# One planned transformer layer on one core: the table of landing times behind the static order is made longer

## The reference, cut to what matters

```
q, k, v = x @ Wq, x @ Wk, x @ Wv              # q and k rotated (rope)
a = softmax(q1 k1' * s + mask) - lam * softmax(q2 k2' * s + mask)
o = a @ v ; group norm over (tokens, 64) of each head ; o @ Wo
x = layernorm(x + o)
W' = clip(round(W / mean|W|), -1, 1) * mean|W|  # W_up, W_gate, W_down
x = layernorm(x + (silu(x @ W_up') * (x @ W_gate')) @ W_down')
```

## Time and profile before

| | |
|---|---|
| median of 3 runs | 2376.57 us (2372.23 to 2381.06) |
| profiled execution, own time | 2373.91 us |
| its span in the trace | 2372.1 us |
| mean granted TensorE clock | 0.989 of full |
| PE busy | 2235.5 us (94%) |
| DVE, ACT, POOL busy | 1715.7 (72%), 1466.9 (62%), 1169.2 us (49%) |
| DMA | 256.54 MB, mean 108 GB/s |

### The profile page before, as it was taken

One profiled execution on the slowest core, in us unless ns is written; L12 is line 12 of the kernel. 1 busy time (PEld: TensorE's weight loads), 2 busy tenths in 40 slices (PEclk: granted clock), 3 DMA queues, 4 the chain that ended last, 5 costly groups with the idle time before them and its releaser, 6 DMA issues.

```text
span 2372.1 us, 41358 instructions
## 1 busy us (share of the span) xinstructions
PE 2235.5 (94%) x13602; PEld 1399.2 (59%) x13602; DVE 1715.7 (72%) x3829; ACT 1466.9 (62%) x3458; POOL 1169.2 (49%) x1919
## 2 busy tenths in 40 slices
PE   8898998989899999999999999999999999999998
PEld 5555565656566666666666666566656666544443
DVE  3676788888778778888877887887777878632343
ACT  1576667666566767676767776677766777521232
POOL 0465657566546545655654454665444454421232
PEclk9899999999999999999999999999999999999999
DMA  6767465656433121424252223252233111102000
GB/s 225 202 208 199 143 208 177 196 182 204 147 100 113 54 74 57 136 72 129 82 162 78 78 80 84 69 168 68 67 121 101 43 52 39 63 23 84 1 18 18
DMA packets 258004, 256.54 MB, mean 108 GB/s; under 512 B 31360, under 2 KB 199424, under 8 KB 255744
## 3 DMA queue, kind: packets, MB, share of 16 engines
q1 hardware_dynamic: 246016, 220.26, 31.0%
q10 hardware_dynamic: 11776, 33.63, 4.5%
HBM read 182.53 MB, written 71.30 MB: 107 GB/s over the span
## 4 chain that ended last, share of the span: by engine, by line
PE 60%; DVE 8%; issue 4%; ACT 3%; POOL 3%; DMA 0%; DVEq 0%; POOLq 0%; ACTq 0%; SPq 0%
PE F L1045 16%; PE F L1032 9%; PE F L1054 8%; PE PV L986 8%; PE S L969 7%; PE F L949 6%; PE F L1012 4%; DVE e_long L1315 2%; ACT dt_long L1103 1%; ACT e_long L1113 1%; DVE e_long L1386 1%; POOL linv L1243 1%; DVE e_short L1386 1%; PE F L953 1%; DVE th L1364 1%
## 5 line engine op out<-in xcount | busy, mean ns | idle before, releaser
L1243 POOL TENSOR_TENSOR linv<-lsum,powers 128x2 f32<-128x2 f32 x512 | 410.5, 802 | 503.0 <-ACT e_long L1113 381.9
L1113 ACT ACTIVATE e_long<-e_long,nmax 128x768 f32<-128x768 f32 (+3 forms) x512 | 504.1, 988 | 127.9 <-DVE nmax L1315 123.8
L1315 DVE CUSTOM_DVE_ANT_0 e_long<-S,mask_b 128x768 f32<-128x768 f32 (+3 forms) x512 | 511.2, 1020 | 95.0 <-PE S L969 90.8
L969 PE MATMUL S<-kstk,qstk 128*128 128x384 f32 (+5 forms) x1536 | 496.8, 421 | 25.7 <-DVE nmax L1315 21.9
L1103 ACT ACTIVATE dt_long<-F 128x512 f32<-128x512 f32 (+3 forms) x544 | 258.5, 516 | 241.1 <-PE F L949 235.3
L969 PEld LDWEIGHTS S<-kstk,qstk 128*128 128x128 f32 x1536 | 274.8, 191 | 164.7 <-issue 83.3
L1386 DVE SCALAR_TENSOR_TENSOR e_long<-e_long,coef 128x1024 f32<-128x1024 f32 (+3 forms) x256 | 277.2, 1083 | 78.1 <-POOL coef L1244 77.5
L1012 PE MATMUL F<-xT,wr 128*128 128x512 f32 x640 | 309.5, 615 | 10.7 <-ACT dt_long L1103 6.8
L1113 ACT ACTIVATE e_short<-e_short,nmax 128x384 f32<-128x384 f32 (+3 forms) x512 | 283.5, 558 | 37.0 <-DVE nmax L1315 36.1
L1256 POOL TENSOR_TENSOR hid<-th,hid 128x512 f16<-128x512 f32 x128 | 148.3, 1159 | 299.4 <-ACT hid L1156 163.8
L1315 DVE CUSTOM_DVE_ANT_0 e_short<-S,mask_b 128x384 f32<-128x384 f32 (+3 forms) x512 | 235.2, 487 | 65.4 <-PE S L969 62.9
(11 more groups left out here) (110 smaller groups left out, 3259.3 us busy)
## 6 DMA issues: line engine op xcount, KB each, us to landing
qstk<-dq SPq DMA_DIRECT2D x512, 128.0 KB, 2.8
dq<-hl SPq DMA_DIRECT2D x32, 1024.0 KB, 4.8
wr<-in_w_proj ACTq DMA_DIRECT2D x48, 512.0 KB, 4.1
kstk<-dk SPq DMA_DIRECT2D x64, 256.0 KB, 5.6
da<-ra SPq DMA_DIRECT2D x32, 512.0 KB, 3.2
at_sb<-da SPq DMA_DIRECT2D x32, 512.0 KB, 4.0
dk<-hl SPq DMA_DIRECT2D x8, 1024.0 KB, 4.7
wt<-in_w_up SPq DMA_DIRECT2D x16, 512.0 KB, 6.2
```

Source lines behind the costliest of these rows:

```text
L969: last = nc.tensor.matmul(slot[:, h, :], qstk[:, duo % 4, 2 * r + m, :].bitcast(F32R), kstk[:, g % 2, m, h * w:(h + 1) * w].bitcast(F32R), ...
L1113: nc.scalar.activation(e, e, ACT.Exp, bias=nmax[:, u % 8:u % 8 + 1], scale=-1.0, accum_out=lsum[:, n % 4, m:m + 1]).then_inc(s_exp, 1)
L1243: link(nc.gpsimd.tensor_tensor(linv[:, a % 8, :], lsum[:, a % 4, :], mone, ALU.pow))
L1315: nc.vector.tensor_tensor_reduce(out, slot, mask, -1.0, -NEG, ALU.add, ALU.min, nmax[:, u % 8:u % 8 + 1]).then_inc(s_negmax, 1)
```

## The change

Two tables of the planner get larger numbers. Nothing else is edited: the same instructions are issued, and what changes is their order on each engine.

```
-HAND_OVER = {"pe": .2, "act": .3, "dve": .2, "pool": .2}
-LANDS = {"load q": 3.1, "load k": 5.5, "load v": 4.5, "store v": 3.9, "store rotated": 5.2, "store a": 3.5, "load a": 4.4,
-         "store out": 2.5, "load wo": 4.0, "load x1": 6.0, "load weight": 4.5, "load x": 3.7, "load w": 4.2, "load rope": 5.0, "load lambda": 5.0, "load first": 2.5}
+HAND_OVER = {"pe": .3, "act": .4, "dve": .3, "pool": .3}
+LANDS = {"load q": 4.5, "load k": 7.5, "load v": 6.0, "store v": 7.0, "store rotated": 6.0, "store a": 4.5, "load a": 6.5,
+         "store out": 2.5, "load wo": 9.0, "load x1": 8.0, "load weight": 12.0, "load x": 6.5, "load w": 6.5, "load rope": 5.0, "load lambda": 6.0, "load first": 2.5}
```

## The result

| | before | changed |
|---|---|---|
| median | 2376.57 us | 2351.28 us (2348.82 to 2355.24, 6 runs) |
| profiled execution, own time | 2373.91 us | 2349.49 us |
| mean granted clock | 0.989 | 0.992 |

The ratio is 0.9895, with a 95% interval of 0.9879 to 0.9911: 25.3 us less by the medians, 24.4 by the profiled executions. The forecast was 2356 us, 21 us less, in a range of 2335 to 2380.

The account below looks back on a forecast made before the run. PE, 94% busy, was taken as the bound, with its idle time and lower clock before 620 us to win. Terms -21 + 1 - 1 = -21 us, from the runs' median 2376.6, gave about 2356 us, range 2335 to 2380.

Parts of the forecast that it names:

- The bound: PE, 94% busy, bounds the kernel; what can be won is 71 us idle and 22 us by clock before 620 us.
- Load weight, -21 us: Batch 0's attention: a later planned landing ends ACT's 17 waits for weight pieces; -21 us, bounds 0 and -28.
- four gaps: PE idle behind ACT's late weight pieces in batch 0: 3.79, 3.45, 5.64 and 2.82 us, together 15.7 us.
- the 25.9 us: Idle time plus clock loss on PE behind the weight waits, of which a share of 0.8 was taken as won.
- the 10.2: Us lost to half clock on PE in the stretches behind the first three gaps, 3.4 us each.
- Load q, load k, store rotated: +1 us: Ahead of the first scores: PE's 1.51 us wait goes, but attention starts up to 4 us later; -1.5 to +4.
- the items put at 0: Store v, loads of x, w, x1 and lambda: no PE wait for them seen; 0, bounds -2 and +4.
- Load a, store a, load wo: -1 us: Ahead of the Wo products: two PE waits go, -3.5 us, longer holes cost 2.5 us; bounds -3.5 and +6.
- Hand-overs: 0, bounds -12 and +12: Every hop of a step planned 0.1 us longer: small waits go or PE is late; 0 taken.
- The waits move: Weight waits vanish but ACT, PE and DVE meet elsewhere in batch 0; 0 to -11 us, 2366 to 2377; chance 0.22.
- The scores come late: Longer hops put scores behind more filling and DVE starves; slower, +11 us if its waits double, up to 2400; chance 0.11.
- The small waits go too: Margins take a third of batch 0's other idle time and clock dips: another -22 us, some 2334; chance 0.15.

Follow-up runs that it names:

- e9: The kernel before with only SP's list changed: each load of a weight piece issued three items earlier; 2357.61 us, ratio 0.9920.
- e4: The kernel before with all landing times of the change except load weight, hand-overs as before; 2384.70 us, ratio 1.0030.
- e3: The kernel before with only the hand-overs raised by 0.1 us; 2388.22 us, ratio 1.0054.
- e1: The kernel before with only load weight raised from 4.5 to 12.0; 2366.38 us, ratio 0.9956.
- e5: The kernel before with load weight at 12.0 and the raised hand-overs, all other landing times old; 2361.72 us, ratio 0.9932.
- e2: The changed kernel with load weight set back to 4.5; 2375.38 us, ratio 0.9988.
- e6: The kernel before with all landing times of the change, load weight included, and hand-overs as before; 2363.99 us, ratio 0.9947.
- e12: The changed kernel with load weight at 8.0 and each load of a weight piece issued two items earlier on SP's list; 2344.95 us, ratio 0.9863.

## Why the prediction was right, point by point

**The bound.** PE's idle time in batch 0 is what moved, as forecast: 17.4 of the 24.4 us lie there. The counts of instructions on the engines are as before. PE's longest wait between 60 and 620 us was 5.64 us and is now 2.15.

**Load weight, -21 us.** This is shown. The waits fell from 38.6 us to none, and the edit is worth 12.0 to 26.5 us in four settings, 20.8 in the mean. With the lists of the four engines held fixed (e9) it is 19.6 us. The sum of the term was near the truth, but its two parts were not sized alike. In the four pairs of the table, by one trace of each kernel, PE's idle time falls by 9.7, 19.2, 12.4 and 18.8 us, 15.0 in the mean, where I had summed 15.7 from four gaps; its busy time changes by +2.1, -5.5, -12.8 and -8.5, 6.2 less in the mean, where I had put 10.2 on the clock.

e9 has the same list on PE as the kernel before, so the two can be laid side by side. Its page has:

```profile
span 2354.8 us, 41358 instructions
...
PE 2230.9 (95%) x13602; PEld 1394.7 (59%) x13602; DVE 1715.7 (73%) x3829; ACT 1465.3 (62%) x3458; POOL 1172.9 (50%) x1919
```

PE's idle time is 123.9 us for 136.6, its busy time 4.6 us less: 17.3 of the 25.9 us came home in this pair of traces, 0.67 of it, where I took 0.8. (The medians are 19.6 us apart; the profiled execution of the kernel before had a clock of 0.989, its other runs lie between 0.984 and 0.989.) Laid side by side item by item, the four gaps gave 3.6, 3.4, 5.5 and 2.1 us, 14.6 in all (from the start of the item ahead of a gap to that of the item behind it, in the one trace and in the other). The stretches behind the first three, from the first product behind the wait to the same later product, stand thus in the kernel before and in e9:

```profile
82.63:89.86 7.23, 7.03 (x41) 5.22 (x42) 2.52 (x7) 4.99 (x14) 3.21 (x5) 0.57 0.01 1
111.83:120.32 8.49, 6.19 (x27) 5.08 (x27) 5.95 (x13) 7.03 (x17) 3.32 (x6) 0.60 0.90 298
210.01:215.82 5.81, 5.81 (x9) 2.50 (x10) 1.28 (x1) 3.34 (x9) 1.27 (x3) 0.55 0.60 141
```

```profile
80.90:86.03 5.13, 4.55 (x41) 3.14 (x42) 3.02 (x10) 5.13 (x14) 4.15 (x5) 1.00 1.04 242
105.23:112.49 7.26, 4.46 (x26) 3.05 (x27) 6.58 (x16) 6.80 (x17) 4.36 (x6) 1.00 1.07 282
197.32:200.57 3.25, 3.25 (x9) 1.52 (x10) 3.05 (x10) 1.84 (x4) 1.27 (x3) 1.00 1.04 300
```

The lower clock is gone from all three, but they are shorter by 2.1, 1.2 and 2.6 us, 5.9 in all, not 10.2. Two things were wrong in the 10.2. The first and the third stretch were taken to begin inside the wait ahead of them (81.90 where PE starts at 82.63, 208.40 where it starts at 210.01), so 2.3 us of idle time, 1.2 us by the clock, stood in both parts of the term. And time at half clock cost less than its length times the missing share where PE, at full clock, waits for others. The third stretch has PE busy throughout in both traces and gave 2.6 us, its length times 0.45. The second gave 1.2 us where its length times 0.40 is 3.4: in e9 PE is idle for 2.8 of its 7.26 us. The first gave 2.1 where its length times 0.43 is 3.1, with 0.6 of 5.13 us idle in e9. So the four gaps and the three stretches gave 20.5 us; some 3 of them were lost elsewhere, 2.3 of them ahead of the first place, where the same scores start at 78.41 us in e9 and at 76.08 in the kernel before.

In the changed kernel itself the split is different again. I had put 0.8 of 15.7, some 13 us, on idle time and 0.8 of 10.2, some 8 us, on the clock; the traces have 22.7 and 1.7. That the total came within 5 us is in part luck: one part was too low and the other too high.

**Load q, load k, store rotated: +1 us.** Here is PE's timeline of the changed kernel ahead of the first scores:

```profile
61.57 1.88 PE L1012 MATMUL F<-xT,wr 128*128 128x512 f32 x4
62.88 1.49 PE L969 MATMUL S<-kstk,qstk 128*128 128x512 f32 x4
```

The wait of 1.51 us is gone and the first scores start 2.3 us later (62.88 for 60.61), behind more projection work. The forecast of its form was right; its worth in the end was not measured alone. Nor was that of the next term: e4, which has this part, the next and the items put at 0 together, lost 6.3 us on the kernel before.

**Load a, store a, load wo: -1 us.** In the changed kernel's timeline the first Wo products of batches 0 and 2 stand thus, against the earlier trace rows:

```profile
589.12 1.98 PE L1032 MATMUL F<-wo_sb,at_sb 128*128 128x512 f32 x4 [0.84 <-DVE t L1350]
...
1782.47 1.88 PE L1032 MATMUL F<-wo_sb,at_sb 128*128 128x512 f32 x4
```

Both waits for Wo's operands are gone; ahead of the first PE now waits 0.84 us for a bank. It comes 41 us earlier, not the 20 that I forecast. The hole ahead of batch 2 is longer, and yet PE is less idle in it. Its busy time from the last down product to Wo, before and changed:

```profile
1749.30:1759.10 9.80, 5.86 (x60) 4.40 (x58) 8.32 (x22) 8.58 (x22) 4.42 (x9) 0.95 0.92 288
```

```profile
1769.00:1782.40 13.40, 11.05 (x83) 8.19 (x81) 10.91 (x27) 10.78 (x27) 6.52 (x14) 0.87 0.81 250
```

Idle are 3.9 us in the one and 2.4 in the other. But the clock is 0.95 in the one and 0.87 in the other, at most another 0.5 and 1.7 us, so the two cost about the same. My price for the hole, 28% of its length, was too high: the 3.94 idle of 14.10 us held the 2.13 us of the wait that the same sum takes off. Without them it is 1.81 of 14.10, 13%.

**Hand-overs: 0, bounds -12 and +12.** On the kernel before they cost 9.8 us (e3), on top of load weight they give 4.7 (e1 to e5), on top of the rest of the landing times 9.3 (e4 to e2), on top of both others 12.7 (e6 to changed). The width was about right, and the 0 too high: the mean is 4.2 us less, of effects of either sign. It is not an effect that is absent.

**The rivals.** "The waits move" was seen in part: in e1, where load weight alone was worth 12 us. "The scores come late" was not seen in the changed kernel: DVE's waits for scores up to 620 us, against the earlier trace rows, are as they were (45.4 for 46.0 us):

```profile
DVE e_long L1315 <- PE S L969: 31.6, 23, 15.4
...
DVE e_short L1315 <- PE S L969: 13.8, 26, 1.6
```

"The small waits go too" holds for some 6 us at most: the 55.3 us of other idle time up to 620 us are 53.6, and behind it 4.2 are gone. I had also forecast PE at over 90% from 60 to 620 us. It is (145.34 + 361.06) / 560 = 90.4%, but only since mixing now begins at 589 us; up to there it is 475.52 of 529.00 us, 89.9%. And the fit weighed there, 2.0 us plus the bytes over 436 GB/s (the Trainium skill, "DMA: Bandwidth & Descriptors", "Anatomy of one DMA — SWDGE (gpsimd) path"), is given for single transfers by another path, and doesn't carry over to these loads under this traffic: by its 3.2 us, an estimate, the old 4.5 would have been ample, and the order planned with it lost 19.6 us that e9 took back.

**What stays open.** Why the changed kernel is 6 us faster than e9 and e12 6 us faster than the changed one is open; that it is other coincidences is a guess. The experiments show that such differences come with every new order, up to some 15 us, and not which item makes them. So the changed kernel's 25.3 us are, by my estimate, about 20 of the weight waits (20.8 and 19.6 above), and some 5 that another order might not have brought.

## What to carry to other kernels

In a static order the landing time to plan with is a late one, not the median: here 16.0 in place of 12.0 cost 3.6 us and 4.5 cost 24.1. An item put too late in the list costs little while there is other work, one put too early stops its engine and all behind it. Look for waits on an engine that is *not* the bound, for a load off the critical path, and then at whether the bound engine's gaps end with the item behind. Before crediting a number in a planner's table, hold the order fixed and move only the transfer, as every new order wins or loses by itself.

## What was not expected of the hardware

Half clock cost its length times the missing share only where PE had no waits at full clock either (2.6 us of 5.81 at a clock of 0.55); where it waits for others at full clock, a stretch of 8.49 us at 0.60 cost 1.2 us and not 3.4. And transfers of one size landed between 3.6 and 10.3 us after issue in the changed kernel (48 loads of 512 KB by SP's queue), a spread that a median of 5.3 hides:

```profile
L905 SPq DMA_DIRECT2D wt<-in_w_up x16: 422/602/2400, 64.2 to 348.6; - x16
...
DMA to landing us min/median/max: 3.6/5.3/10.3
```
